# Two tile pairs of the first group by Strassen's product, with thresholds moved to ScalarE and copies reordered, in a fused AdaLN and ternary feed-forward kernel

## The reference, cut to what matters

```
x [16, 256, 512], cond [16, 256]          # 16 batches of 256 tokens
q_emb = relu(cond @ W3 + b3)              # [16, 512]
y  = (256 * x + sum_tokens(x)) * q_emb    # per batch
h  = relu(y @ W2 + b2)                    # [16, 256, 512]
h_q = 0.5 where h > 0.33, else 0          # ternary, but h is never negative
w_q = 0.6 where weight > 0.2, -0.6 where weight < -0.2, else 0
out = x + h_q @ (w_q + rram).T
```

## Time and profile before

| | |
|---|---|
| time, median of 3 runs | 173.18 us (172.96 to 173.58) |
| the profiled execution's own time | 173.29 us |
| its span | 171.3 us |
| TensorE matmul busy | 165.5 us, 97% |
| VectorE busy | 131.5 us, 77% |
| ScalarE busy | 71.6 us, 42% |
| GpSimd busy | 85.4 us, 50% |
| share of the chain that ended last | PE 82%, DVE 6%, ACT 3%, issue 2% |

### The profile page before, as it was taken

How to read it: one execution, slowest core, us unless ns; L and a number is a source line. 1 busy time by engine, 2 the same in 40 slices (tenths; PEclk the granted TensorE clock), 3 DMA queues, 4 the chain that set the end, 5 groups by cost and what they waited for, 6 DMA issues and landing times.

```text
span 171.3 us, 2197 instructions
## 1 busy us (share of the span) xinstructions
PE 165.5 (97%) x684; PEld 120.6 (70%) x684; DVE 131.5 (77%) x202; ACT 71.6 (42%) x177; POOL 85.4 (50%) x85
## 2 busy tenths in 40 slices
PE   7989999999999999999999999999999999999991
PEld 2889787777653478686654459997654459999991
DVE  3589999998998999683968998778636167776751
ACT  2159776955302259999107996532000001001000
POOL 3000950669005492470089302758099203999990
PEclk9999999999999999999999999999999999999998
DMA  5999999998600394819949005983293000343166
GB/s 161 239 241 232 243 218 234 221 231 197 122 0 0 89 382 116 152 46 250 405 128 376 19 0 141 339 322 124 85 334 132 0 4 4 120 182 130 65 252 234
DMA packets 31211, 28.99 MB, mean 169 GB/s; under 512 B 1600, under 2 KB 22368, under 8 KB 31200
## 3 DMA queue, kind: packets, MB, share of 16 engines
q1 hardware_dynamic: 30128, 28.07, 60.0%
q10 hardware_dynamic: 1008, 0.79, 1.7%
q0 software_dynamic: 64, 0.00, 0.0%
HBM read 20.47 MB, written 8.39 MB: 168 GB/s over the span
## 4 chain that ended last, share of the span: by engine, by line
PE 82%; DVE 6%; ACT 3%; issue 2%; DVEq 0%; ACTq 0%
PE out_ps L964 12%; PE hid_ps L964 10%; PE out_ps L941 9%; PE out_ps L1028 8%; PE hid_ps L873 6%; PE hid_ps L866 6%; PE hid_ps L934 5%; PE hid_ps L915 5%; PE hid_ps L927 5%; PE hid_ps L907 5%; PE hid_ps L890 5%; PE hid_ps L1020 4%; ACT t_sum L470 2%; PE hid_ps L941 2%; DVE xT L539 1%
## 5 line engine op out<-in xcount | busy, mean ns | idle before, releaser
L433 ACT ACTIVATE xT<-xT,coef,q_scale 128x256 f32<-128x256 f32 x64 | 34.0, 596 | 8.5 <-DVE coef L556 4.5
L539 DVE STREAM_TRANSPOSE xT<-x_in 128x1024 f32<-128x1024 f32 x15 | 30.7, 2054 | 0.0
L439 ACT ACTIVATE junk<-xT,q_emb 128x256 bf16<-128x256 f32 x40 | 19.8, 499 | 14.8 <-DVE xT L539 14.7
L373 POOL TENSOR_TENSOR x_res<-x_res,pieces 128x256 f32<-128x256 f32 x8 | 5.9, 742 | 24.2 <-DVE x_res L713 24.2
L493 ACT ACTIVATE pieces<-out_ps 128x256 f32<-128x256 f32 x6 | 2.3, 383 | 31.8 <-PE out_ps L964 29.8
L1028 PE MATMUL out_ps<-xT,w_sb 128*128 128x512 f32 x32 | 13.9, 592 | 0.0
L379 POOL TENSOR_TENSOR x_res<-x_res,pieces 128x256 f32<-128x256 f32 x16 | 13.5, 870 | 0.0
L941 PE MATMUL out_ps<-wT_lo,hid 128*128 128x512 f32 x32 | 13.3, 415 | 0.0
L941 PE MATMUL out_ps<-wT_hi,hid 128*128 128x512 f32 x32 | 12.5, 390 | 0.0
L1028 PEld LDWEIGHTS out_ps<-xT,w_sb 128*128 128x128 f32 x32 | 9.8, 309 | 3.6
L362 POOL TENSOR_TENSOR a_sum<-hid 128x1024 fp32r<-128x1024 f32 x2 | 4.7, 2347 | 14.6 <-DVE t_sum L618 14.6
(11 more groups left out here) (135 smaller groups left out, 413.7 us busy)
## 6 DMA issues: line engine op xcount, KB each, us to landing
x_in<-in_x SPq DMA_DIRECT2D x24, 256.0 KB, 5.3
x_res<-in_x SPq DMA_DIRECT2D x3, 2048.0 KB, 9.1
out<-x_res SPq DMA_DIRECT2D x24, 256.0 KB, 3.5
x_in<-in_x SPq DMA_DIRECT2D x1, 2048.0 KB, 9.5
out<-x_in SPq DMA_DIRECT2D x7, 256.0 KB, 2.1
x_in<-in_x SPq DMA_DIRECT2D x12, 128.0 KB, 6.4
w_sb<-in_L_cond_W SPq DMA_DIRECT2D x4, 256.0 KB, 6.7
x_res<-in_L_ffn_weight SPq DMA_DIRECT2D x4, 256.0 KB, 6.6
```

The lines of the kernel that those rows point to most:

```text
L433: nc.scalar.activation(part, part, ACT.Identity, bias=coef[:, n, k:k + 1], scale=q_scale[:, n, k:k + 1]).then_inc(s_xs, 1)
L539: nc.vector.transpose(xT[:, s, :, cols].rearrange("p j (n t) -> p n j t", t=BLK), x_in[:, p % SLOTS, b * NB:(b + 1) * NB].rearrange("p n ( ...
```

## The change

- `PAIRS_OF[0]` is no longer empty: tiles 2, 6 and 3, 7 of group 0 become pairs 2 and 3 of `project_pair`. Tiles 0, 1, 4, 5 (`DIRECT`) stay with `project`. Pairs are now counted by `pair_number`, with these two as numbers 0 and 1.
- The thresholds of group 0's second half (batches 2 and 3, four banks) leave VectorE (`quantize(1, m)`) for ScalarE: a Sign with the bias b2 - 0.33, and a Relu of it.
- GpSimd makes `a_sum` for the two new pairs (`hidden_sums(0)`) ahead of `wT_lo`, and adds their pieces behind `b_lo`.
- ScalarE makes `b_hi` in two halves around the sum of batch 8. Batch 11 is no longer summed on ScalarE: VectorE sums it by chunks behind the two pairs, and ScalarE scales it behind `copy_p1(2, 0)` and `copy_p1(2, 1)`.
- ScalarE interleaves the gathers of W2 columns with the scaling of batch 1.
- On TensorE `p3(1, 1)` comes after two direct tiles, not four. The waits for pair banks now stand in group 2 as well.

```diff
-    PAIRS_OF = (0, 4, 4, 3)
+    PAIRS_OF = (range(2, 4), range(4), range(4), range(3))
     TILES = 8
-    CHUNK_SUMS = (0, 1, 3)
+    DIRECT = (0, 1, 4, 5)
+    CHUNK_SUMS = (0, 1, 3, 11)
...
+        def pair_number(g, c):
+            return 4 * g + c - 2
...
+            def hidden_sums(g):
+                cols = slice(2 * P, TOK) if g == 0 else slice(0, TOK)
+                h = hid[:, g % 2].bitcast(F32)
+                left, right = h[:, :, 0:TOK][:, :, cols], h[:, :, TOK:][:, :, cols]
+                a11, a12, a21, a22 = left[:, 0:2], left[:, 2:4], right[:, 0:2], right[:, 2:4]
+                sums, out_sums = a_sum[:].bitcast(F32)[:, :, :, cols], a_sum[:, :, :, cols]
+                if g == 0:
+                    pool.wait_ge(s_cls_hid, KD)
+                    pool.wait_ge(s_cls_hid2, KD)
+                else:
+                    pool.wait_ge(s_c11, 2 * g)
+                    pool.wait_ge(s_c12, 2 * g)
+                    pool.wait_ge(s_c21, 2 * g)
+                    pool.wait_ge(s_c22, 2 * g)
+                    pool.wait_ge(s_pp[7], pair_number(g, 0))
+                nc.gpsimd.tensor_tensor(out_sums[:, 0], a21, a22, ALU.add).then_inc(s_asum, 1)
+                pool.wait_ge(s_asum, 4 * g + 1)
+                nc.gpsimd.tensor_tensor(out_sums[:, 1], sums[:, 0], a11, ALU.subtract).then_inc(s_asum, 1)
+                nc.gpsimd.tensor_tensor(out_sums[:, 2], a11, a21, ALU.subtract).then_inc(s_asum, 1)
+                pool.wait_ge(s_asum, 4 * g + 2)
+                nc.gpsimd.tensor_tensor(out_sums[:, 3], a12, sums[:, 1], ALU.subtract).then_inc(s_asum, 1)
...
-            for i in range(4):
+            for i in (0, 1, 3, 2):
                 pool.wait_ge(s_bhi, i + 1)
                 nc.gpsimd.tensor_tensor(b_lo[:, i], b_sum[:, i], b_hi[:, i].bitcast(F32), ALU.subtract).then_inc(s_blo, 1)
...
+            for c in PAIRS_OF[0]:
+                add_pieces(0, c)
             pool.wait_ge(s_tsum, 8)
             hidden_sums(1)
...
+            gather_columns(0)
+            gather_columns(1)
+            scale_chunk(1, 0)
+            gather_columns(2)
+            scale_chunk(1, 1)
+            gather_columns(3)
+            scale_chunk(1, 2)
+            scale_chunk(1, 3)
             scale_summed(2)
...
+            act.wait_ge(s_th, 2)
+            for m in range(KD):
+                act.wait_ge(s_cls, KD + m + 1)
+                if m > 0:
+                    act.wait_ge(s_cls_hid2, m)
+                nc.scalar.activation(sign[:], out_ps[m][:], ACT.Sign, bias=bias_col[:, m:m + 1]).then_inc(s_sign, 1)
+                act.wait_ge(s_sign, m + 1)
+                nc.scalar.activation(hid[:, 0, m, TOK:], sign[:], ACT.Relu).then_inc(s_cls_hid2, 1)
             for h, cols in enumerate(COLS):
                 act.wait_ge(s_wT, h + 1)
                 nc.scalar.copy(wT_hi[:, :, cols], wT[:, :, cols]).then_inc(s_whi, 1)
...
+            weight_sum_hi(0)
+            weight_sum_hi(1)
+            act.wait_ge(s_tr, 8)
+            accumulate(8)
+            weight_sum_hi(2)
+            weight_sum_hi(3)
+            scale(8)
+            act.wait_ge(s_tr, 9)
+            accumulate(9, (0, 1))
+            copy_pair_p1(0, 2)
+            accumulate(9, (2, 3))
+            scale(9)
+            copy_pair_p1(0, 3)
             sum_and_scale(10)
-            sum_and_scale(11)
             copy_p1(2, 0)
             copy_p1(2, 1)
+            for k in range(KD):
+                scale_chunk(11, k)
             sum_and_scale(12)
...
+            nc.vector.tensor_scalar(bias_col[:], b2_col[:], TH_X, None, ALU.subtract).then_inc(s_th, 1)
...
-            quantize(1, 0)
...
-            for m in range(1, KD):
-                quantize(1, m)
...
             finish(0)
             finish(1)
+            c12(1, 1)
             finish(2)
+            finish(3)
+            pair_c22(0, 2)
+            pair_u2(0, 2)
             transpose_batch(10)
-            finish(3)
-            c12(1, 1)
-            finish(4)
-            transpose_batch(11)
-            for c in range(5, TILES):
-                finish(c)
+            pair_c21(0, 2)
+            pair_c11(0, 2)
+            pair_c12(0, 2)
+            pair_u3(0, 2)
+            finish_pair(0, 3)
+            prepare_by_chunks(11)
...
-            def wait_pair_banks(b):
-                pe.wait_ge((s_o21, s_o11, s_o12, s_u3)[b], 4)
+            def wait_pair_banks(g, b):
+                pe.wait_ge((s_o21, s_o11, s_o12, s_u3)[b], pair_number(g - 2, 3) + 1)
...
+                if g > 0:
+                    wait_hidden(g + 1 if c == 1 and g < LAST else g)
+                elif c == 3:
+                    wait_hidden(1)
                 if u == 0:
-                    pe.wait_ge(s_out, TILES)
+                    pe.wait_ge(s_out, 1)
                 if u >= 2:
                     pe.wait_ge(s_o11, u - 1)
                 pair_product(1, u, 0, h[:, top], block(top, left), True, False, first)
                 pe.wait_ge(s_asum, summed + 1)
-                pe.wait_ge(s_blo, 4)
+                pe.wait_ge(s_blo, 1)
+                if u == 0:
+                    pe.wait_ge(s_out, 3)
                 if u >= 2:
                     pe.wait_ge(s_o12, u - 1)
                 pair_product(5, u, 2, a_sum[:, 0], t_sum_of(0), True, False, first)
                 pe.wait_ge(s_asum, summed + 2)
+                pe.wait_ge(s_blo, 2)
                 if u >= 2:
                     pe.wait_ge(s_u3, u - 1)
                 pair_product(6, u, 1, a_sum[:, 1], t_sum_of(1), True, False, first)
+                pe.wait_ge(s_blo, 3)
+                if u == 0:
+                    pe.wait_ge(s_out, len(DIRECT))
                 if u >= 2:
                     pe.wait_ge(s_o21, u - 1)
                 pair_product(4, u, 3, h[:, bottom], t_sum_of(3), True, True, second)
...
             project(0)
             project(1)
+            p3(1, 1)
             project(2)
             project(3)
-            p3(1, 1)
-            for c in range(4, TILES):
-                project(c)
+            for c in PAIRS_OF[0]:
+                project_pair(0, c)
```

More of the change, by code:

```diff
@@ L127, in adaln_ffn_kernel @@
         th_col = sbuf("th_col", [P, KD])
+        bias_col = sbuf("bias_col", [P, KD])
+        sign = sbuf("sign", [P, TOK])
         warm = sbuf("warm", [P, D], mybir.dt.bfloat16)
@@ L240, in store @@
                 for n, c in enumerate(tiles):
-                    sp.wait_ge(s_out, (TILES if g == LAST else 0) + n + 1)
+                    sp.wait_ge(s_out, (len(DIRECT) if g == LAST else 0) + n + 1)
                     sp.dma_start(out_tiles[g * TILES + c], res[g][:, c]).then_inc(s_stored[g], DMA)
             def store_pairs(g):
-                for c in range(PAIRS_OF[g]):
-                    u = 4 * (g - 1) + c
+                for c in PAIRS_OF[g]:
+                    u = pair_number(g, c)
                     sp.wait_ge(s_r12, u + 1)
@@ L284, in _ @@
             load_pair(7)
-            store(0, range(TILES))
+            store(0, DIRECT)
+            store_pairs(0)
             sp.wait_ge(s_stored[0], DMA * TILES)
@@ L415, in _ @@
             last_hidden_sums(2)
-            for c in range(PAIRS_OF[LAST]):
+            for c in PAIRS_OF[LAST]:
                 add_pieces(LAST, c)
@@ L467, in _, with gather_columns @@
                 scale_chunk(0, k)
-            for k in range(KD):
+            def gather_columns(k):
                 act.wait_ge(s_w2[k], DMA)
                 nc.scalar.copy(w2_col[:, k], w2_sb[:, k].rearrange("p (c m) -> p m c", m=KD)).then_inc(s_w2_col, 1)
-            for k in range(KD):
-                scale_chunk(1, k)
+            gather_columns(0)
[6 more added lines that the diff above has]
+            scale_chunk(1, 3)
             scale_summed(2)
@@ L519, in _ @@
             for g in (2, LAST):
-                for c in range(PAIRS_OF[g]):
+                for c in PAIRS_OF[g]:
                     copy_pair_p1(g, c)
             for h, cols in enumerate(COLS):
-                act.wait_ge(s_out, TILES + 2 + h)
+                act.wait_ge(s_out, len(DIRECT) + 2 + h)
                 act.dma_start(out_tiles[LAST * TILES + TILES - 1, :, cols], res[LAST][:, TILES - 1, cols]
@@ L722, in pair_u3, with finish_pair @@
                                                ALU.mult, ALU.add).then_inc(s_u3, 1)
-            def finish_pairs(g):
[L725 to L729, removed]
-                    pair_c12(g, c)
-                    pair_u3(g, c)
+            def finish_pair(g, c):
+                pair_c22(g, c)
+                pair_u2(g, c)
+                pair_c21(g, c)
+                pair_c11(g, c)
+                pair_c12(g, c)
+                pair_u3(g, c)
+            def finish_pairs(g):
+                for c in PAIRS_OF[g]:
+                    finish_pair(g, c)
             def transpose_weight(h):
@@ L1070, in _ @@
                     project_pair(g - 1, c)
-            for c in range(PAIRS_OF[LAST]):
+            for c in PAIRS_OF[LAST]:
```

(6 more changed lines are left out.)

103 lines of the change are left out of this document (45 added, 58 removed).

## The result

The changed kernel took 174.19 us (median of 20 executions, 173.26 to 175.44), the kernel before 173.24 us (20, 172.92 to 174.13) beside it. The ratio is 1.0046, 95% interval 1.0029 to 1.0063: slower by 0.8 us (the two medians lie 0.95 us apart), where 0.24 us less was forecast. The profiled execution's span went from 171.3 to 172.2 us.

The account below looks back on a forecast made before the run. TensorE was taken as the bound, its matmuls covering 97% of the span. Terms -0.52 - 0.59 + 0.10 + 0.77 = -0.24 us gave 172.9 us, no change that shows; own range 172.6 to 173.5, with rivals 171.8 to 174.0.

Parts of the forecast that it names:

- The start: Batch 1's wave: with gathers spread, TensorE goes on at 17.49, not 18.01; -0.52 us, bound 0 if a later place swallowed it.
- Group 2: Batch 11's later scaling delays the first token sum, so `sum_167` starts at S + 14.81, not S + 14.04: +0.77 us.
- T: Start of group 2's first token sum, forecast 6.09 us behind the start of group 2, at 82.84.
- the four thresholds that leave VectorE: Group 0's second-half thresholds, gone from VectorE: claimed to bring nothing, since TensorE did not wait for VectorE there.
- The pairs: Group 0's output: four direct tiles at 7.31 us become two pairs at 3.36, -0.59, plus 0.10 (0 to 0.25) for waiting.
- Behind group 2: After `sum_167` the same 10.80 us follow, and groups 2 and 3 are otherwise untouched: 0.
- ScalarE's time for the thresholds: Eight new ScalarE operations from 44.36, 0.64 us each, 5.1 us in all; direct tiles do not wait: cost nothing.
- GpSimd's sums ahead of `wT_lo`: Four sums at 1.29 us each until 54.7; the second `wT_lo` ends at 59.8, 1.1 us ahead of the direct tiles: nothing.
- the residual loads: Group 1's residual load goes later, at 92.2, and lands at 101.3, wanted at 103.4; 2.1 us spare: nothing.
- the coefficients of batch 11: VectorE's four small operations behind the second pair, possibly locked out by GpSimd's additions; counted as nothing.
- The rival on GpSimd and the coefficients: GpSimd's late additions meet batch 11's coefficients, delaying group 2's token sum: +1.7 - 0.24, some 174.6 us; chance 0.08.
- The chance of 0.22 for slower: Whole kernel slower: 0.12 for dear ScalarE thresholds, 0.08 for GpSimd's additions meeting the coefficients, 0.02 more.

Follow-up runs that it names:

- e3: The changed kernel with batch 11's first scaling moved between the two copies of p1 of group 2; 173.55 us, ratio 1.0008 to the kernel before.
- e11: e6 with both copies of p1 of group 1 ahead of batch 7's scaling on ScalarE; 173.29 us, ratio 0.9973 to the kernel before.
- e12: The same kernel as e6, timed and profiled again; 172.97 us, ratio 0.9972 to the kernel before.
- e9: The changed kernel itself, timed and profiled again; 173.98 us, ratio 1.0028 to the kernel before.
- e4: The changed kernel with group 0's residual load in two, tiles 4 to 7 loaded earlier; 173.96 us, ratio 1.0026 to the kernel before.
- e1: The kernel before with only the gathers of W2 columns spread among batch 1's scalings; 173.11 us, ratio 0.9985.
- e2: The changed kernel with the four gathers of W2 columns together again ahead of the scalings; 174.12 us, ratio 1.0032 to the kernel before.
- e8: The kernel before with only batch 11 changed: summed by chunks on VectorE, scaled on ScalarE behind both copies of p1; 174.20 us, ratio 1.0039.
- e5: The changed kernel without the pairs, all eight tiles of group 0 direct again; 174.48 us, ratio 1.0052 to the kernel before.
- e6: The changed kernel with VectorE's transposes of batches 10 and 11 earlier and three batch 11 scalings ahead of p1's second copy; 172.15 us, ratio 0.9915 to the kernel before.
- e10: The kernel before with only the thresholds of group 0's second half moved to ScalarE; 173.14 us, ratio 0.9990.

## Why the prediction was wrong

- **The start, -0.52 forecast, nothing in the sum.** This is the step that failed. In the profile of the changed kernel the direct tiles begin 0.14 us later than before, not 0.52 earlier. "I see none up to the output tiles" overlooked three waits that stood just behind the one removed. First, the W2 chunks: in the profiles of the changed kernel, e3, e11 and e12 the second half of batch 0's products waits for one, until 13.97, 13.67, 13.60 and 14.31, so the wave begins late whatever ScalarE does. Second, p2 of group 1 behind batch 7's coefficient (e9, and e3, where p2 resumes at 43.90). Third, GpSimd's last weight sum and the first token sum of group 1 run into each other: the token sum took 2.37 us in the changed kernel, where it took 1.23 in e9 and e4. The changed kernel's profile has the first and the third: its wave ends 0.20 us earlier than before (24.98 for 25.18), and from p1 of group 1 to the direct tiles 0.34 us are lost again (22.85 for 22.51), nearly all where p7 waits for `sum_16`, which follows the token sum. Which of the waits strikes differs from execution to execution; that the landing of the loads decides it is what the profiles suggest, and no run moved a load of the start alone. e1's interval holds everything from 0.66 us gained to 0.14 lost, and e2 shows no gain in the changed kernel.
- **Group 2, +0.77 forecast, +1.07 measured.** The mechanism was right: e8 has it alone, e5 without the pairs, e3 moves it one to one. In all ten profiles of kernels that scale batch 11 behind the first copy of p1, with that sum starting from 4.94 us (e6) to 6.18 us (e2, e9) behind p1, the length of group 2 less the token sum's start is the same, 19.73 to 19.79 us. Of the miss of 0.30 us, 0.08 is the token sum itself, 6.17 us behind p1 for 6.09. The other 0.22 is what a real wait costs TensorE, which was mis-sized. I had p7 through at T + 8.6, just ahead of VectorE's own T + 8.72; worked back from `sum_16`'s end, that gives the signal 0.05 us and the product 1.76, as p7 to `sum_167` in the earlier trace rows. In the changed kernel p7 starts 0.15 us behind the end of `sum_16` (90.48 to 90.63), and its result is taken 1.99 us later (92.62, T + 8.94), 0.19 us after VectorE was free for it. So `sum_167` came 15.11 us behind p1 instead of 14.81, and the same 10.80 us follow. I was also wrong that the four thresholds that leave VectorE bring nothing: e10 alone makes group 2 0.27 us shorter. In the changed kernel this can't be seen, since the later token sum sets the length there. The changed kernel with batch 11 left in its old place was not run.
- **The pairs, -0.49 forecast, -0.39 measured** (15.93 for 16.32 us). The second pair took 3.51 us for 3.35: 0.16 us, within what I allowed (0 to 0.25). The place was right too: its p3 starts at 76.31, 0.14 us behind the end of `pair_c22`, where I gave the signal 0.05. The direct tiles cost 7.35 for 7.30.
- **Behind group 2, 0 forecast, +0.07 measured:** the first pair takes 3.42 us for 3.35. ScalarE comes late to its copy of that pair's first product, behind the scaling of batch 14 (1.31 us behind the pair's start, 0.96 before), and VectorE's second addition waits 0.24 us for it.
- **Costed at nothing and rightly so:** ScalarE's time for the thresholds (0.67 and 0.63 us each, 5.7 us in all; direct tiles not waiting), GpSimd's sums ahead of `wT_lo`, the residual loads (e4), and the coefficients of batch 11, which took 0.16 us each. The rival on GpSimd and the coefficients looked at the wrong place: what GpSimd held up in the changed kernel was the first token sum of group 1.

With the measured terms: -0.39 + 1.07 + 0.07 = +0.75, and 0.14 from the stretch ahead of the direct tiles, is 0.89, the difference of the two ends. The chance of 0.22 for slower was too small: with the start at nothing, which was named as its bound, my own other terms already add up to +0.28 us.

## What to carry to other kernels

Before counting a removed wait as gained, look for the second-latest thing at that place, and at the places behind it that have hardly more slack than the wait gives: here the second p2 had 0.54 us to its copy, and 0.52 us were to be gained. Transposes put where VectorE is idle waiting for a load, with the scalings that they make possible (e6), took 1.20 us off group 2, three times what the two pairs gave. Where a queue is in order, count the slack to the first use from the start of the stage, and keep it under what the stage allows. Here that is some 4.8 us, an estimate: the shortest group 2, e10's 24.57, less the 19.76 us that follow the token sum's start. 5.1 us are enough to be no worse than the kernel before, and 6.17 cost 1.07 us.

## What the runs showed of the hardware

In the changed kernel the first token sum of group 1 took 2.37 us beside GpSimd's sums, not 1.23. The Trainium skill has it so (SBUF — State Buffer, Who interferes with whom): a VectorE instruction with two SBUF inputs contends with a GpSimd instruction that reads SBUF. The trace adds that a large operation can lose nearly its whole own length: it starts at 42.84, and GpSimd's four sums run from 39.14 to 44.12.

```profile
42.84 2.37 DVE L650 TENSOR_TENSOR t_sum<-xT 128x1024 f32<-128x1024 f32 x1 [1.16 <-ACT xT L452]
```

```profile
39.14 4.98 POOL L339 TENSOR_TENSOR x_res<-x_res 128x512 f32<-128x512 f32 x4 [1.94 <-DMA x_res<-in_L_ffn_rram_variation]
```

It ends at 45.21, 1.09 us after GpSimd is through, so nearly all of its own 1.23 us of work was done after that. The same sum took 2.36 or 2.37 us in e2, e3, e6, e10 and e12 too, and in all six profiles it started 1.27 to 1.28 us ahead of GpSimd's end, as the fourth sum began. It took 1.23 us in the other seven, where it started 0.04 to 0.07 us ahead of that end.

The start of batch 1's wave lay between 17.02 and 18.25 us in twelve of the thirteen profiles, in four of them behind a W2 chunk that ended a wait of TensorE at 13.60 to 14.31. The thirteenth, e10's 19.08, had some 3.4 us at the lower granted clock. Seven of the timed executions have a mean granted clock of 0.976 to 0.978, and each took 0.95 to 1.61 us more than the median of its kernel. But at a mean clock of 1.0 the changed kernel's times still go from 173.97 to 175.12 us, so the clock is one part of the scatter and not all of it.
